# A sparse graph layer: x held for 20 tiles in five blocks, results written over x, x and out moved in blocks of four tiles

## The chip, the cores and the metric

The kernel runs on one core of a Trainium2 chip. The metric is the device time of one execution in microseconds (us). The kernel before took 1267.18 us, the median of 3 runs (1265.48 to 1268.1). All numbers are 32-bit floats.

The core has five instruction streams that run beside each other and meet at semaphores: PE (matrix products), DVE (vector work), ACT (activation functions and scaled copies), POOL (here it issues the gathers) and SP (here it issues all other transfers). Sixteen DMA engines carry the transfers of all of them.

## The reference

x is 8192 x 512, adj is 8192 x 8192. An entry of adj is nonzero with a chance of about 0.1%, and on the whole diagonal.

```python
h = jnp.maximum(_layernorm(x, axis=-1), 0.0)
head = (adj > 0).astype(adj.dtype)
head = head / jnp.maximum(jnp.sqrt(jnp.sum(head * head, axis=-1, keepdims=True)), 1e-12)
inc = adj + head
out = x + (inc @ h) / jnp.sum(inc, axis=-1, keepdims=True)
```

So every row of the result is its row of x plus a weighted mean of some nine rows of h.

## The kernel before, in words

**The tiling.** x is cut into 16 blocks of 512 rows. A block is 128 lanes of four rows in a row, so that one lane's part of a block is 8 KB that lie together in memory. A tile is one row of each lane of a block (128 rows; 2 KB in each lane, with 8 KB from lane to lane in memory), and there are 64 tiles, four to a block.

**First stage.** `ln_load` (L372) brings the blocks of x, DVE and ACT normalize them, and `ln_store` (L376) writes h to a scratch in memory. The first `HELD_CHUNKS` blocks land in `held`, which keeps them; the others land in space that the gathers use later.

**Second stage, one period for each tile t.** SP loads the tile's 128 rows of adj, 4 MB, as four transfers of 1 MB (L385) into one of two buffers. DVE folds the halves of a row together (L774), takes the eight largest of each quarter (L779) and their places (L783). From these it works out columns and weights. POOL gathers 8 rows of h for each lane by slot (L488, `slot_column`), and further rows, the spill, by 3 more transfers (L488, `spill_column`). PE multiplies them by diagonal and spill matrices and adds them up in one of three accumulators `acc`. The last three tiles and a batch of rows that the quick way missed go slightly other ways.

**The order is written out by hand.** Each engine has a `period(t)` with the steps of several tiles: DVE and ACT search and check tile t, while weights of t-1, products of t-2 and the spill of t-3 and t-4 are done in between. PE's period begins with `product_spill(t-4)` (L1341), then `residual(t-2)`, which starts the accumulator with x by a product with the unit matrix (L1318), then `bring_spill(t-2)` (L1301), on whose result DVE's `find_entry` (L941) waits one period later.

**Where x is used again.** A tile's rows of x are needed twice: by PE's `residual`, and by ACT's `row_again` (L642), which rebuilds the tile's own rows of h. For tiles 0 to 15 they come from `held`. For the 48 others `load_x(t)` (L392) brings 256 KB into one of two buffers `x_residual`, two periods ahead; it waits until PE and ACT have used the tile two before.

**The way out.** ACT's `finish_tile(t)` (L649) copies the accumulator to one of two buffers `out_tile`, once the store of two tiles before has landed. SP's `store_tile(t)` (L396) writes it, 256 KB, as a part of period t+4.

**SP's queue.** All transfers but the gathers go through SP in one order. In period t: quarters 0 and 1 of adj tile t+2, the store of tile t-4, the load of x for tile t, quarters 2 and 3. A quarter is issued when ACT has checked it in tile t and DVE has folded it. What waits at SP's head holds all that is behind it.

## Time and profile before

| | |
|---|---|
| median of 3 runs | 1267.18 us |
| the profiled execution, whole | 1265.03 us |
| its span in the trace | 1263.2 us |
| DVE busy | 1162.8 us, 92% |
| ACT and PE busy | 977.8 and 970.4 us, 77% each |
| POOL busy | 764.9 us, 61% |
| moved by the DMA engines | 471.29 MB, 373 GB/s over the span |

How to read it: the span is the time between the first and the last instruction of the trace. The 1.83 us between span and whole execution are start and end. Busy shares are means over three stages. The first 100 us are the normalization, some 100 to 1150 us are the tiles' periods, and the rest is the end, where the last tiles drain. In the second stage DVE and the DMA engines are both near their limits.

### The profile page before, as it was taken

Reading aid. Unit: us, or ns where it says so; the run is one execution under the profiler, and the core shown is the slowest. Engines: PE = TensorE matmul, PEld = TensorE weight load, DVE = VectorE, ACT = ScalarE, POOL = GpSimd, SP = SyncE. Lnnn points to the kernel's source line nnn. Section 1 sums busy time; section 2 is a strip of 40 time slices with the busy share of each in tenths; the row PEclk is TensorE's granted clock in tenths of the full one; section 3 lists DMA queues with packets and bytes.
Section 4 is the critical chain, followed back from the end, with each engine's and each line's share of the span. In section 5 each row is a group of like instructions: output and inputs, shape, how many; then the busy total and the mean of one; then the engine's idle time right before and its main releaser. Section 6 shows DMA issues by size and latency. Waiting matters only on the chain.

```text
span 1263.2 us, 14630 instructions
## 1 busy us (share of the span) xinstructions
PE 970.4 (77%) x2678; PEld 482.8 (38%) x2678; DVE 1162.8 (92%) x2794; ACT 977.8 (77%) x1903; POOL 764.9 (61%) x745
## 2 busy tenths in 40 slices
PE   0002889988888888888888888798888878878676
PEld 0001334444444434444433444344444434434343
DVE  6679999999999999999998999989999989998972
ACT  6657888898888887888887787788878778876551
POOL 1003666766666667676666666775666667667453
PEclk9999999888889999889988988988899889998698
DMA  9999999999999999999999999999999999999442
GB/s 360 428 421 406 398 402 392 392 394 399 396 391 402 401 399 398 384 401 394 384 398 368 400 398 391 388 395 373 402 400 400 385 382 387 398 399 355 142 143 79
DMA packets 148127, 471.29 MB, mean 373 GB/s; under 512 B 24386, under 2 KB 24386, under 8 KB 143876
## 3 DMA queue, kind: packets, MB, share of 16 engines
q1 hardware_dynamic: 90368, 331.38, 66.9%
q0 software_dynamic: 57664, 138.93, 29.9%
q8 instruction: 25, 0.41, 0.1%
q14 instruction: 70, 0.57, 0.1%
HBM read 490.21 MB, written 33.82 MB: 415 GB/s over the span
## 4 chain that ended last, share of the span: by engine, by line
DVE 45%; DMA 20%; issue 20%; ACT 5%; SPq 5%; another core or an unknown queue 2%; PE 1%; DVEq 0%; ACTq 0%; POOL 0%; POOLq 0%
DMA adj_tile<-in_adj_dram 17%; DVE folded L774 15%; DVE cand_word L779 12%; DVE cand_index L783 5%; DMA gathered_rows<-in_x_dram 3%; SPq L385 2%; ACT junk L569 2%; DVE cand_word L797 2%; SPq L392 2%; DVE cand_index L802 2%; ACT adj_tile L556 2%; SPq L396 1%; DVE ln_stats L757 1%; DVE weights_and_payload L914 1%
## 5 line engine op out<-in xcount | busy, mean ns | idle before, releaser
L488 POOL DMA_INDIRECT gathered_rows<-h_scratch,slot_column x520 | 536.8, 1032 | 265.9 <-issue 161.2
L569 ACT ACTIVATE junk<-adj_tile,zero_unit 128x2048 bf16<-128x2048 f32 x256 | 510.1, 1994 | 111.2 <-issue 75.5
L1330 PE MATMUL acc<-gathered_rows,diag 128*128 128x512 f32 x1040 | 504.1, 641 | 0.5 <-issue 0.5
L488 POOL DMA_INDIRECT gathered_rows<-h_scratch,spill_column x197 | 220.5, 1119 | 199.0 <-ACT spill_column L615 150.8
L774 DVE SCALAR_TENSOR_TENSOR folded<-adj_tile 128x1024 f32<-128x1024 f32 x248 | 301.4, 1215 | 12.1 <-DMA adj_tile<-in_adj_dram 10.7
L1330 PEld LDWEIGHTS acc<-gathered_rows,diag 128*128 128x128 f32 x1040 | 213.7, 212 | 247.1 <-issue 246.8
L779 DVE MAX8 cand_word<-folded 128x8 f32<-128x1024 f32 x248 | 302.9, 1221 | 2.2
L783 DVE FIND_INDEX8 cand_index<-cand_word,folded 128x8 uint32<-128x1024 f32 x248 | 302.2, 1218 | 0.0
L1341 PE MATMUL acc<-gathered_rows,spill_matrix 128*128 128x512 f32 x394 | 186.3, 607 | 14.6 <-issue 10.7
L632 ACT ACTIVATE diag<-ident,weights_and_payload 128x128 f32<-128x128 f32 x582 | 176.2, 387 | 0.5 <-DVE weights_and_payload L914 0.5
L1278 PE MATMUL poff<-spill_rank,lanes_before 128*128 128x1 f32 x130 | 26.4, 272 | 187.5 <-DVE spill_rank L859 174.4
L1278 PEld LDWEIGHTS poff<-spill_rank,lanes_before 128*128 128x128 f32 x130 | 25.4, 227 | 239.8 <-issue 139.7
L1341 PEld LDWEIGHTS acc<-gathered_rows,spill_matrix 128*128 128x128 f32 x394 | 73.9, 194 | 103.0 <-issue 102.9
L1323 PE MATMUL acc<-own_row,diag 128*128 128x512 f32 x124 | 75.2, 691 | 45.4 <-ACT own_row L642 29.2
L1307 PE MATMUL pturned<-ident,owner 128*128 128x128 f32 x394 | 79.2, 355 | 0.0
L1301 PE MATMUL pbrought<-weights_and_payload,owner 128*128 128x72 f32 (+1 forms) x386 | 71.4, 333 | 3.5 <-ACT owner L607 3.3
L1307 PEld LDWEIGHTS pturned<-ident,owner 128*128 128x128 f32 x394 | 68.8, 257 | 0.0
L615 ACT ACTIVATE spill_column<-entry 128x3 uint32<-128x3 f32 (+1 forms) x65 | 12.8, 198 | 72.3 <-issue 44.1
L1318 PE MATMUL acc<-x_residual,ident 128*128 128x512 f32 x96 | 53.2, 637 | 17.9 <-issue 14.3
L1301 PEld LDWEIGHTS pbrought<-weights_and_payload,owner 128*128 128x128 f32 x386 | 62.5, 239 | 5.9 <-ACT owner L607 4.5
L623 ACT ACTIVATE spill_matrix<-pturned,entry 128x128 f32<-128x128 f32 x197 | 56.6, 356 | 3.9 <-remote 3.9
L1323 PEld LDWEIGHTS acc<-own_row,diag 128*128 128x128 f32 x124 | 23.1, 211 | 88.1 <-ACT diag L632 46.0
(146 smaller groups left out, 829.8 us busy)
## 6 DMA issues: line engine op xcount, KB each, us to landing
adj_tile<-in_adj_dram SPq DMA_DIRECT2D x256, 1024.0 KB
h_scratch<-adj_tile SPq DMA_DIRECT2D x16, 1024.0 KB, 10.5
out_dram<-out_tile SPq DMA_DIRECT2D x64, 256.0 KB
gathered_rows<-in_x_dram SPq DMA_DIRECT2D x12, 1024.0 KB, 12.6
x_residual<-in_x_dram SPq DMA_DIRECT2D x48, 256.0 KB
gathered_rows<-h_scratch,slot_column POOLq DMA_INDIRECT x520
x_held<-in_x_dram SPq DMA_DIRECT2D x4, 1024.0 KB, 7.9
gathered_rows<-h_scratch,spill_column POOLq DMA_INDIRECT x197
```

Of the source, the lines that this page charges most:

```text
L488: nc.gpsimd.indirect_dma_start(out=into, out_offset=None, in_=h[:, :], in_offset=bass.IndirectOffsetOnAxis(ap=column, axis=0), bounds_chec ...
L569: nc.scalar.activation(junk[:, n % 2].rearrange("p (j c) -> p j c", j=2), both[:, :, half], ACT.Relu, bias=zero_unit[:], scale=-UP, accum_ ...
L623: last = nc.scalar.activation(W[:, t % 2, g], pturned[:, g * P:(g + 1) * P], ACT.Copy, scale=entry[:, t % 2, g, 0:1])
L632: last = nc.scalar.activation(diag[:, t % 2, s], ident[:], ACT.Copy, scale=wpay[:, t % 2, s:s + 1])
L774: nc.vector.scalar_tensor_tensor(out=F[:, j % 2], in0=a[:, 1], scalar=UP, in1=a[:, 0], op0=ALU.mult, op1=ALU.add).then_inc(folded, 1)
L779: nc.vector.max(out=cv[:, t % 2, 8 * j:8 * j + 8], in_=F[:, j % 2]).then_inc(vals_found, 1)
L783: nc.vector.max_index(out=ci[:, t % 2, 8 * j:8 * j + 8], in_max=cv[:, t % 2, 8 * j:8 * j + 8], in_values=F[:, j % 2]).then_inc(idx_found, 1)
L1301: last = nc.tensor.matmul(bank[:, c:c + 3 * n], owner[:, g * P:(g + 1) * P], wpay[:, t % 2, 1 + OWN:1 + OWN + 3 * n], start=True, stop=True)
L1307: last = nc.tensor.matmul(pturned[:, g * P:(g + 1) * P], owner[:, g * P:(g + 1) * P], ident[:], start=True, stop=True)
L1323: nc.tensor.matmul(acc[t % 3][:], diag[:, t % 2, 0], again[:], start=False, stop=False).then_inc(row_added, 1)
L1330: last = nc.tensor.matmul(acc[t % 3][:], diag[:, t % 2, 1 + s], slot(t % 2, s), start=False, stop=False)
L1341: last = nc.tensor.matmul(acc[t % 3][:], W[:, t % 2, g], slot(t % 2, OWN + g), start=False, stop=(g == groups(t) - 1))
```

## The change

- `held` grows from 16 to 20 tiles (five blocks), and `x_residual` and `out_tile` go. A tile's x always lies in `held[:, t % 20]`.
- `finish_tile` writes the result over the tile's x in `held`. It waits for no store any more. The batch's result goes to `again`.
- The store is of a whole block: 1 MB, 8 KB in a row in each lane, issued by SP in every fourth period, from t = 8. It waits until the block's four tiles are finished.
- x comes again in whole blocks as well, for blocks 5 to 15, eleven transfers of 1 MB. Block c+5 goes over block c and waits until the store of c has landed; SP issues it two periods after that store. So the loads lie in periods 10, 14, ... 50.
- PE tells nobody any more that x is used (`res_added` is gone).

```diff
-    HELD_CHUNKS = 4
+    HELD_CHUNKS = 5
...
-        held = sb("x_held", [P, HELD, D], fp32)
-        xres = sb("x_residual", [P, 2, D], fp32)
+        held = sb("x_then_out", [P, HELD, D], fp32)
         again = sb("own_row", [P, D], fp32)
-        osb = sb("out_tile", [P, 2, D], fp32)
...
         def x_of(t):
-            return held[:, t] if t < HELD else xres[:, t % 2]
+            return held[:, t % HELD]
+        def group(c):
+            k = c % HELD_CHUNKS
+            return held[:, ROWS * k:ROWS * (k + 1), :]
+        def out_of(t):
+            return again[:] if t == BATCH else held[:, t % HELD]
+        def x_come(t):
+            c = t // ROWS
+            return x_loaded[c % 2], 16 * ((c - HELD_CHUNKS) // 2 + 1)
...
-            def load_x(t):
-                if t >= HELD + 2:
-                    sp.wait_ge(res_added, t - 1)
-                    if not wide(t - 2):
-                        sp.wait_ge(row_ready, t - 1)
-                sp.dma_start(xres[:, t % 2], x_t[t // ROWS, t % ROWS]).then_inc(x_loaded[t % 2], 16)
-            def store_tile(t):
-                sp.wait_ge(out_ready, t + 1)
-                sp.dma_start(out_t[t // ROWS, t % ROWS], osb[:, t % 2]).then_inc(out_stored[t % 2], 16)
+            def load_x(c):
+                sp.wait_ge(out_stored[(c - HELD_CHUNKS) % 2], 16 * ((c - HELD_CHUNKS) // 2 + 1))
+                sp.dma_start(group(c), x_ln[c]).then_inc(x_loaded[c % 2], 16)
+            def store_group(c):
+                sp.wait_ge(out_ready, ROWS * c + ROWS)
+                sp.dma_start(out_ln[c], group(c)).then_inc(out_stored[c % 2], 16)
...
-                if t >= 4:
-                    store_tile(t - 4)
-                if t >= HELD:
-                    load_x(t)
+                if t >= 2 * ROWS and t % ROWS == 0:
+                    store_group(t // ROWS - 2)
+                if t % ROWS == 2 and HELD_CHUNKS <= t // ROWS - 2 + HELD_CHUNKS < LN:
+                    load_x(t // ROWS - 2 + HELD_CHUNKS)
...
-            for t in range(TILES - 4, TILES):
-                store_tile(t)
+            for c in range(LN - 2, LN):
+                store_group(c)
...
             def finish_tile(t):
                 act.wait_ge(acc_ready, t + 1)
-                if t >= 2:
-                    act.wait_ge(out_stored[t % 2], 16 * (t // 2))
-                nc.scalar.activation(osb[:, t % 2], acc[t % 3][:], ACT.Copy).then_inc(out_ready, 1)
+                nc.scalar.activation(out_of(t), acc[t % 3][:], ACT.Copy).then_inc(out_ready, 1)
```

In `row_again` and `residual` the wait for `x_loaded` takes its semaphore and count from `x_come(t)`. The compute engines keep their orders; what moves stands in SP's queue. Before, around the period in which the first x is loaded again (a quarter of adj is one L385, and `out_ready` is ACT's finished tile):

```order
L385 DMA adj_tile<-in_adj_dram 128x2x1024 [waits folded,checked] x4
L396 DMA out_dram<-out_tile 128x512 [waits out_ready]
L392 DMA x_residual<-in_x_dram 128x512
L385 DMA adj_tile<-in_adj_dram 128x2x1024 [waits folded,checked] x4
L396 DMA out_dram<-out_tile 128x512 [waits out_ready]
L392 DMA x_residual<-in_x_dram 128x512
L385 DMA adj_tile<-in_adj_dram 128x2x1024 [waits folded,checked] x4
L396 DMA out_dram<-out_tile 128x512 [waits out_ready]
L392 DMA x_residual<-in_x_dram 128x512 [waits row_ready,res_added]
L385 DMA adj_tile<-in_adj_dram 128x2x1024 [waits folded,checked] x4
```

Now, from the second tile's quarters to the second store (the first rows are periods 0 to 8; `out_stored` is the store's landing):

```order
L389 DMA adj_tile<-in_adj_dram 128x2x1024 [waits folded,checked] x34
L398 DMA out_dram<-x_then_out 128x2048 [waits out_ready]
L389 DMA adj_tile<-in_adj_dram 128x2x1024 [waits folded,checked] x8
L394 DMA x_then_out<-in_x_dram 128x2048 [waits out_stored0]
L389 DMA adj_tile<-in_adj_dram 128x2x1024 [waits folded,checked] x8
L398 DMA out_dram<-x_then_out 128x2048 [waits out_ready]
```

Two transfers of 256 KB between four quarters of adj have become one transfer of 1 MB between eight, a store and a load by turns, and eight quarters stand between a store and the load that waits for its landing.

On ACT, before, in a period of the second stage (L649 is `finish_tile`, L642 is `row_again`):

```order
L569 ACTIVATE junk,zero_units<-adj_tile,zero_unit 128x2048 [waits adj_loaded13,adj_loaded12,checked]
L649 ACTIVATE out_tile<-acc1 128x512 [waits out_stored1,acc_ready]
L593 ACTIVATE half_minus_offset<-poff 128x1 [waits places_paid,reach_ready,offset_ready]
L594 ACTIVATE spill_end<-poff,spill_rank 128x1
L600 ACTIVATE from_first_place<-place_number,half_minus_offset 128x384 [waits owner_found,minus_ready]
```

And now, at the same place:

```order
L571 ACTIVATE junk,zero_units<-adj_tile,zero_unit 128x2048 [waits adj_loaded13,adj_loaded12,checked]
L649 ACTIVATE x_then_out<-acc1 128x512 [waits acc_ready]
L595 ACTIVATE half_minus_offset<-poff 128x1 [waits places_paid,reach_ready,offset_ready]
L596 ACTIVATE spill_end<-poff,spill_rank 128x1
L602 ACTIVATE from_first_place<-place_number,half_minus_offset 128x384 [waits owner_found,minus_ready]
```

Nothing has moved there; the wait of L649 for a store is gone.

## Rows read from the trace of the kernel before

**Rows 1.** The page, part 1: busy us, share of the span, instructions of each engine.
```profile
PE 970.4 (77%) x2678; PEld 482.8 (38%) x2678; DVE 1162.8 (92%) x2794; ACT 977.8 (77%) x1903; POOL 764.9 (61%) x745
```
**Rows 2.** Stretches: busy us (instructions) of PE, PEld, DVE, ACT, POOL; clock, DMA share, GB/s.
```profile
100.00:350.00 250.00, 202.76 (x564) 102.39 (x565) 248.46 (x585) 210.97 (x410) 164.22 (x158) 0.92 1.02 397
350.00:400.00 50.00, 45.58 (x132) 22.91 (x131) 49.69 (x117) 42.57 (x85) 34.09 (x34) 0.93 1.02 395
400.00:1150.00 750.00, 640.58 (x1761) 316.88 (x1760) 718.76 (x1689) 612.91 (x1206) 506.11 (x474) 0.90 1.02 392
1000.00:1050.00 50.00, 42.67 (x114) 21.24 (x114) 44.89 (x107) 39.85 (x80) 33.68 (x33) 0.90 1.01 378
1050.00:1100.00 50.00, 43.47 (x124) 21.75 (x122) 49.69 (x118) 41.53 (x80) 33.73 (x33) 0.93 1.03 400
```
**Rows 3.** SP in time, before x is loaded again: start, us, instruction, count.
```profile
209.31 0.36 SPq L396 DMA_DIRECT2D out_dram<-out_tile  x1
...
226.00 0.36 SPq L396 DMA_DIRECT2D out_dram<-out_tile  x1
228.70 12.40 SPq L385 DMA_DIRECT2D adj_tile<-in_adj_dram  x4
```
**Rows 4.** SP in time, later, a period with a load of x.
```profile
741.64 2.07 SPq L396 DMA_DIRECT2D out_dram<-out_tile  x1
743.80 1.77 SPq L392 DMA_DIRECT2D x_residual<-in_x_dram  x1
745.67 11.66 SPq L385 DMA_DIRECT2D adj_tile<-in_adj_dram  x4
```
**Rows 5.** Waits from 150 to 1150 us: waiter, releaser, us in total, times, longest.
```profile
DVE own_entry L941 <- remote: 13.0, 3, 5.0
...
ACT half_minus_offset L593 <- remote: 11.5, 3, 4.4
...
DVE folded L774 <- DMA adj_tile<-in_adj_dram: 6.8, 9, 1.5
...
PE acc L1318 <- DMA x_residual<-in_x_dram: 3.5, 3, 1.8
```
**Rows 6.** ACT in time, 1018 to 1024 us; in brackets the idle time before.
```profile
1018.36 0.57 ACT L649 ACTIVATE out_tile<-acc 128x512 f32<-128x512 f32 x1
1023.34 0.17 ACT L593 ACTIVATE half_minus_offset<-poff 128x1 f32<-128x1 f32 x1 [4.40 <-remote]
```
**Rows 7.** The chain of waits, 930 to 975 us: start, us, what.
```profile
939.71 24.45 DMA adj_tile<-in_adj_dram
```
**Rows 8.** The page, part 6: DMA issues, count, KB each.
```profile
out_dram<-out_tile SPq DMA_DIRECT2D x64, 256.0 KB
...
x_residual<-in_x_dram SPq DMA_DIRECT2D x48, 256.0 KB
```
**Rows 9.** The page, part 3: SP's queue: packets, MB, share of 16 engines.
```profile
q1 hardware_dynamic: 90368, 331.38, 66.9%
```
**Rows 10.** The same queue from 20 to 60 us (blocks of x and h only).
```profile
q1 hardware_dynamic: 2347, 17.06, 101.1%
```
**Rows 11.** SP's queue and the gathers' from 100 to 350 us.
```profile
q1 hardware_dynamic: 18859, 69.33, 70.6%
q0 software_dynamic: 12316, 29.72, 31.7%
```
**Rows 12.** POOL in time: the last spill gather of a period.
```profile
719.28 1.36 POOL L488 DMA_INDIRECT gathered_rows<-h_scratch,spill_column  x1 [0.30 <-issue]
```
**Rows 13.** PE in time: the product that waits for it.
```profile
727.08 2.81 PE L1341 MATMUL acc<-gathered_rows,spill_matrix 128*128 128x512 f32 x6
```
**Rows 14.** Line L396: count, duration ns min/median/max, first and last start.
```profile
L396 SPq DMA_DIRECT2D out_dram<-out_tile x64: 332/734/3240, 159.3 to 1249.0; - x64
```
**Rows 15.** The chain of waits, from 1240 us.
```profile
1253.88 0.61 ACT out_tile L649
```
**Rows 16.** The chain of waits, first 10 us: a block of x, 1 MB, with no other transfer done.
```profile
0.80 4.84 DMA x_held<-in_x_dram
```

More of the change, by code:

```diff
@@ L66, in add_graph_layer @@
     x_ln = x.rearrange("(c p j) d -> c p j d", p=P, j=ROWS)
-    x_t = x.rearrange("(c p j) d -> c j p d", p=P, j=ROWS)
-    out_t = out.rearrange("(c p j) d -> c j p d", p=P, j=ROWS)
+    out_ln = out.rearrange("(c p j) d -> c p j d", p=P, j=ROWS)
     adj_h = adj.rearrange("(c p j) (h n) -> c j p h n", p=P, j=ROWS, h=2)
@@ L314, in add_graph_layer @@
         spill_gathered = [sem(f"spill_gathered{b}") for b in range(2)]
-        res_added = sem("res_added")
         row_added = sem("row_added")
@@ L422, in _ @@
                     load_chunk(t + 2, 3)
-            for t in range(TILES - 4, TILES):
-                store_tile(t)
+            for c in range(LN - 2, LN):
+                store_group(c)
             for b in range(2):
-                sp.wait_ge(out_stored[b], 16 * (TILES // 2))
+                sp.wait_ge(out_stored[b], 16 * (LN // 2))
             sp.wait_ge(list_ready, 1)
@@ L434, in _ @@
                     sp.dma_start(A[:, 0, :], adj[bass.ds(row, P, step=ROWS), :]).then_inc(d_adj, 16)
-                    sp.dma_start(xres[:, 0], x[bass.ds(row, P, step=ROWS), :]).then_inc(d_x, 16)
+                    sp.dma_start(held[:, 0], x[bass.ds(row, P, step=ROWS), :]).then_inc(d_x, 16)
                     for c in range(NCH):
@@ L440, in _ @@
                     sp.wait_ge(d_out, j + 1)
-                    sp.dma_start(out[bass.ds(row, P, step=ROWS), :], osb[:, 0]).then_inc(d_stored, 16)
+                    sp.dma_start(out[bass.ds(row, P, step=ROWS), :], held[:, 1]).then_inc(d_stored, 16)
                     sp.wait_ge(d_stored, j * 16 + 16)
@@ L536, in _ @@
             for b in range(2):
-                pool.wait_ge(out_stored[b], 16 * (TILES // 2))
+                pool.wait_ge(out_stored[b], 16 * (LN // 2))
             pool.wait_ge(out_ready, BATCH + 1)
@@ L540, in _ @@
                 out=out[:, :], out_offset=bass.IndirectOffsetOnAxis(ap=bad_row[:, 0:1], axis=0),
-                in_=osb[:, 0], in_offset=None,
+                in_=out_of(BATCH), in_offset=None,
                 bounds_check=N - 1, oob_is_err=False).then_inc(batch_stored, 16)
@@ L639, in row_again @@
                 if t >= HELD:
-                    act.wait_ge(x_loaded[t % 2], 16 * x_turn(t))
+                    act.wait_ge(*x_come(t))
                 c, j = t // ROWS, t % ROWS
@@ L1265, in _ @@
                     dve.wait_ge(d_x, j * 16 + 16)
-                    nc.vector.scalar_tensor_tensor(out=osb[:, 0], in0=pdense[:], scalar=drd[:], in1=xres[:, 0],
+                    nc.vector.scalar_tensor_tensor(out=held[:, 1], in0=pdense[:], scalar=drd[:], in1=held[:, 0],
                                                    op0=ALU.mult, op1=ALU.add).then_inc(d_out, 1)
@@ L1316, in residual @@
                 elif t >= HELD:
-                    pe.wait_ge(x_loaded[t % 2], 16 * x_turn(t))
-                nc.tensor.matmul(acc[t % 3][:], ident[:], again[:] if t == BATCH else x_of(t), start=True,
-                                 stop=False).then_inc(res_added, 1)
+                    pe.wait_ge(*x_come(t))
+                nc.tensor.matmul(acc[t % 3][:], ident[:], again[:] if t == BATCH else x_of(t), start=True, stop=False)
                 if not wide(t):
```

2 lines of the change are left out of this document (removed).

## The prediction, made before the changed kernel was run

> **What bounds the kernel now.** I read the page's busy times first. DVE is busy for 92% of the span and no other engine for more than 77% [rows 1], so DVE is the first suspect. A mean says nothing of stages, so next I cut the span into stretches [rows 2]. From 100 to 350 us DVE is busy for 248.46 of 250 us, 99.4%: it is the bound, and a gap of 0.6% is what its instructions leave between them. From 400 to 1150 us it is busy for 718.76 of 750 us. At 99.4% it would be 745.4, so 26.6 us are lost there. They come in lumps: 44.89 of 50 us from 1000 to 1050, and the full 49.69 from 1050 to 1100.
>
> What sets in after 350 us? Tile 16 is the first whose x must be loaded again. SP's queue shows what that does. Before it, a store is handed over in 0.36 us, and SP then waits until the next quarter of adj may go [rows 3]. Later the same hand-over takes 2.07 us, that of x 1.77, and the next quarters follow at once [rows 4]: SP's queue is full and SP is held by it. The DMA engines are busy at a share of 1.02 in both stretches [rows 2], so the share doesn't tell them apart; SP's hand-over time does. The waits then name the forms in which the loss reaches DVE and ACT [rows 5]: quarters of adj that come late (6.8 us), PE's brought entries that come late (13.0 us in three waits), and behind these ACT steps that start late (11.5 us in three, one of 4.40 us right behind a finished tile [rows 6], whose cause the trace doesn't name). PE waits for x by name only 3.5 us. The chain of waits passes through quarters of adj that need 24.45 us from issue to landing [rows 7].
>
> So: up to about 360 us DVE is the bound and the DMA engines just keep up. From then on the DMA engines are the bound, by a little. A period in which DVE rules is 16.69 us by the spacing of SP's stores, 226.00 minus 209.31 [rows 3]. The 750 us hold about 43.4 periods (750 minus 26.6, by 16.69), so each is 26.6 / 43.4 = 0.61 us too long: the DMA engines need 17.30 us for a tile with its x and its store.
>
> **What the change takes from the DMA engines.**
> - Bytes: x comes again for 44 tiles instead of 48, 1.05 MB less of 471 MB.
> - Packets: 48 + 64 = 112 transfers of 256 KB [rows 8] with 2 KB in a row are 14336 packets. They become 11 + 16 = 27 transfers of 1 MB with 8 KB in a row, 3456 packets: 10880 fewer. SP issues 400 transfers in all; their data packets by the access patterns are 83968 (65536 of 4 KB for adj, 4096 of 8 KB, 14336 of 2 KB), and the queue counts 90368 [rows 9], so every transfer adds 16 small ones. 85 transfers fewer are 1360 of these. Together 12240 fewer.
>
> What is a packet worth? The trace has stretches of different mix. SP's queue from 20 to 60 us, almost all 8 KB: 101.1% of 16 x 40 us is 647 us of engine time for 17.06 MB, 37.9 us per MB at 138 packets per MB [rows 10]. From 100 to 350 us, 4 KB for the most part: 2824 us for 69.33 MB, 40.7 us per MB at 272 [rows 11]. That gives 2.8 us for 134 packets, 21 ns each. The gathers of the same 250 us: 1268 us for 29.72 MB, 42.7 us per MB at 414 [rows 11], which against SP's queue gives 1.9 us for 142 packets, 14 ns each. The second pair is taken in one and the same stretch, under one load, so I take 14 ns. The upper end is 21 ns. The lower end is 0: the first pair also differs in what runs beside it, and neither pair holds a 2 KB packet by itself.
>
> The Trainium skill, "DMA: Bandwidth & Descriptors", section "Why small descriptors are slow", speaks against so large a price: it gives about 3 cycles for a packet inside a DMA engine, and the same page an 850 MHz fabric, so 3.5 ns as an estimate. The rows show 14 and 21 ns between mixes, so the trace doesn't agree so far, but it doesn't isolate the packet either. With 3.5 ns the gain below would be about 4 us.
>
> **The sum.** In the second stage each tile has, per tile, 2 x (128 - 32) = 192 data packets and 2 x 16 - 16 / 2 = 24 small ones fewer, 216 x 14 ns / 16 engines = 0.19 us. The excess over DVE's period falls from 0.61 to 0.42 us. It now falls on 44 tiles (periods 10 to 53) instead of 48: the fifth block moves the start of the loading, and the ten last periods have none. 44 x 0.42 = 18.5 us. Before, loading began at 360 us and from 350 to 400 DVE still has its 49.69 us [rows 2], so about four periods, 2.4 us, were absorbed by what had been loaded ahead. The same lead is there again: 16.1 us remain of 26.6. Gain 10.5 us.
>
> With 0 ns a packet: 44 x 0.61 - 2.4 = 24.4, gain 2.2 us. With 21 ns: 44 x 0.33 - 2.4 = 12.1, gain 14.5 us.
>
> What lies beside other work and costs nothing:
> - ACT's copy over x and PE's product keep their size, and ACT and PE are busy for 77%. Nothing reads a tile's x after its accumulator is done.
> - ACT's wait for a store goes. No row names it as the one that ended last, so it is worth 0.
> - SP's added wait, a load of block c+5 for the landing of store c: two periods, 33 us, lie between the two issues, and a transfer in the full queue needs about 24.5 us [rows 7]. So 9 us are to spare. If they were not, every quarter of adj behind would be held, and DVE after it.
> - x now lies in `held` some 12 periods before it is used, where the load had been issued two periods before. The 3.5 us of named waits go [rows 5], but they are one form of the same lack and not added.
> - First stage: the fifth block lands in `held` instead of the gathers' space. The stores of h pace those loads. 0.
>
> **The end.** The last store is issued at 1249.0 us [rows 14]; the batch's result is finished at 1254.5 [rows 15], and POOL sends it after both. The last store grows from 256 KB to 1 MB. Alone, 1 MB needs 4.84 us [rows 16], so it lands at 1253.9, in time; beside the last gathers it may need up to 3 us more, a cost of 0 to 2.4. I take 0.5, since the nearest row is the lone transfer.
>
> Total: 10.5 - 0.5 = 10.0 us. Against the profiled execution that is 1265.03 - 10.0 = 1255.0. The median of the runs shown lies 2.15 above it, so I forecast 1267.18 - 10.0 = 1257.2 us.
>
> **The rivals.**
> - *A packet costs next to nothing.* Then only the bytes and the four tiles count: 2.2 - 0.5, or 1265.5 us. For it: no row isolates a 2 KB packet. Against it: both pairs of rows give 14 ns or more. Chance 0.13.
> - *The loss is not the engines' throughput but late x and the small buffers around it.* Then it goes wholly: 26.6 us, at most 1240.6 us. For it: the loss begins with the loads of x, and two tiles of lead are little against 24.5 us of latency. Against it: SP is held in handing over adj as well, which a late x alone wouldn't do. Chance of ending below 1249: 0.12.
> - *The bursts stall DVE.* A period with a block's transfer asks for 0.75 MB more than a mean one. A tile without x and store needs 17.30 less 2 x 0.7 = 15.9 us of DMA time (262 KB at 43 us per MB by 16 engines is 0.7), one with a block 15.9 + 2.5 = 18.4, so 1.7 us over DVE's period. If nothing is given back in the light periods, 22 such periods cost 38 us instead of 26.6: 1267.2 + 11.4 = 1278.6 us. It decides when the lead of the adj loads is under 1.7 us. Against it: quarters are in flight for 24 us, and in a light period the full queue gains 0.8 us again. Chance 0.07.
> - *Gathers wait behind large packets.* If an engine takes packets of both queues by turns, a gather waits 8 KB x 37.9 us per MB = 0.31 us for each of its own instead of 0.17, for the 8 packets that an engine has of a block: 1.1 us, in 27 transfers. The last spill gather is handed over at 720.6 and its product starts at 727.1 [rows 12, 13], so several us are to spare in a calm period, but none in the three lumps. If half of the bursts meet no slack, 15 us are added, 1272 us. Chance 0.05. The skill's same page, "Queues, rings and completion order", says that an engine goes round its queues packet by packet; no row shows the turn itself.
>
> **How the numbers follow.** Forecast (a gain between 3 and 18 us) 0.63; the others 0.13, 0.12, 0.07, 0.05. The measurement tells 0.2%, 2.5 us, from no change. Faster: 0.63 + 0.12 + 0.02 of the first rival = 0.77. Within 0.2%: 0.11. Slower: 0.12 from the two last. The forecast's own range is 1249 to 1264. The range of eight in ten takes in the first rival and part of the second: 1247 to 1267.
>
> **What would show it.** Right: DVE's busy time from 400 to 1150 us rises to some 730 to 738 of 750; SP's queue holds about 78100 packets and some 330 MB; the cost per MB of that queue falls in the second stage; SP is still held in its hand-overs of adj from about 270 us on; the x loads' waits are gone. Wrong: DVE's busy time stays near 719 with fewer packets (a packet was cheap, or the lumps have a cause of their own); SP's load of a block waits for the store's landing; adj is waited for in every fourth period; or POOL's last send moves behind the last store.

## The result: 0.5% slower, and the profile after

The changed kernel took 1273.06 us, the median of 5 runs (1269.94 to 1274.22), against 1267.18 us before (5 runs by now, 1263.14 to 1268.1, the same median): a ratio of 1.0047, 95% interval 1.0027 to 1.0066. Forecast were 1257.2 us and a range of 1247 to 1267. Put on other chips beside the kernel before, the changed kernel had 1.0018 (1.0007 to 1.0030) and 1.0030 (1.0008 to 1.0051). The three intervals overlap, the first two barely; the times differ by up to 16 us, since the chips differ (below). So it is slower by 2 to 6 us, where 10 us less were forecast.

The page of the changed kernel, parts 1 and 3. It answers to [rows 1, 9].

```profile
span 1271.3 us, 14427 instructions
...
PE 974.2 (77%) x2677; PEld 486.8 (38%) x2678; DVE 1163.8 (92%) x2794; ACT 976.3 (77%) x1903; POOL 772.2 (61%) x745
...
DMA packets 135886, 470.23 MB, mean 370 GB/s; under 512 B 23026, under 2 KB 23026, under 8 KB 128180
...
q1 hardware_dynamic: 78128, 330.32, 66.0%
```

The packets are as counted, 78128 on SP's queue, and the engines' time for that queue fell: 66.0% of 1271.3 us is 839.1 us, against 66.9% of 1263.2, 845.1 us [rows 9]. That is 6.0 us of DMA time less, and the span is 8.1 us longer. So the DMA engines have less to do, and DVE still waits longer. Stretches of the changed kernel, columns as in [rows 2]:

```profile
100.00:350.00 250.00, 204.77 (x571) 102.07 (x572) 248.46 (x583) 208.34 (x399) 164.10 (x158) 0.92 1.02 394
350.00:400.00 50.00, 42.31 (x119) 21.43 (x117) 48.88 (x115) 40.69 (x84) 34.84 (x31) 0.90 1.03 401
400.00:1150.00 750.00, 637.23 (x1751) 320.31 (x1752) 711.39 (x1665) 609.71 (x1203) 507.68 (x472) 0.88 1.01 388
...
1100.00:1150.00 50.00, 44.43 (x125) 21.51 (x124) 49.69 (x118) 42.53 (x85) 34.18 (x33) 0.90 1.01 379
```

From 350 to 400 us DVE now loses time (48.88 instead of 49.69), from 400 to 1150 it has 711.39 us instead of 718.76 [rows 2], and from 1100 to 1150 it has its full 49.69 us at 379 GB/s. At 99.4% DVE would have 745.4 us from 400 to 1150, so it loses 34.0 us there, where the prediction's sum had 16.1 for the whole stage. The kernel before, from 1100 to 1150 us, lost 0.6 us, with more bytes moved:

```profile
1100.00:1150.00 50.00, 43.00 (x118) 21.80 (x119) 49.10 (x120) 42.80 (x85) 33.78 (x32) 0.86 1.02 396
```

The shortage starts earlier. In both traces it ends before the stage does: the last big wait of DVE is over at 1029 us before the change (the ACT step ahead of it is in [rows 6]) and at 1072 us now, and the tiles that follow run at DVE's own pace. The waits of the changed kernel from 150 to 1150 us, answering to [rows 5]:

```profile
DVE own_entry L941 <- remote: 14.9, 4, 5.1
ACT junk L571 <- DMA adj_tile<-in_adj_dram: 14.9, 10, 3.5
ACT half_minus_offset L595 <- remote: 11.1, 4, 4.9
...
DVE folded L774 <- issue: 6.4, 7, 1.7
```

The forms are the same as before; PE's named wait for x is gone. In this trace the lumps sit at the block transfers: ACT stands from 745, 851 and 1061 us, and SP began a block at 742, 850 and 1059. (In `after_third` it stands from 1071 and 1110 us with the last block begun at 1058, so it isn't a rule.) SP in time, 736 to 756 us (start, us, instruction), answering to [rows 4]:

```profile
741.08 0.88 SPq L389 DMA_DIRECT2D adj_tile<-in_adj_dram  x2
742.01 6.72 SPq L394 DMA_DIRECT2D x_then_out<-in_x_dram  x1
752.94 1.60 SPq L389 DMA_DIRECT2D adj_tile<-in_adj_dram  x2
```

ACT in the same stretch, answering to [rows 6]:

```profile
744.64 0.57 ACT L649 ACTIVATE x_then_out<-acc 128x512 f32<-128x512 f32 x1
750.11 0.17 ACT L595 ACTIVATE half_minus_offset<-poff 128x1 f32<-128x1 f32 x1 [4.89 <-remote]
```

SP needs 6.72 us to hand over one block of x; ACT then stands for 4.89 us at the same step as before.

**The end.** The chain of waits of the changed kernel, from 1250 us (start, us, what), answering to [rows 15]:

```profile
1250.39 6.42 DMA gathered_rows<-h_scratch,spill_column
1256.81 0.14 issue
1256.94 5.47 PE acc L1340 x6
...
1262.44 0.61 ACT own_row L649
```

The last block is stored from 1250.91 us, half a microsecond after this gather. In this execution the gather took 6.42 us and the last product waited for it. In a later execution of the same kernel (`after_third`) the chain's end passes from product to product without such a wait, and its stretch from 1250 us is like that of [rows 15]:

```profile
1253.25 2.59 PE acc L1340 x6
1255.84 0.02 issue
1255.86 0.61 ACT own_row L649
```

So the end may cost between nothing and a few us; these are two executions on two chips.

### The profile page after: what moved, and what is told of

Same layout as the page of the kernel before. It is cut to its first block, busy times and chain, and to the rows that moved or that the text cites. A ratio compares the mean times of both kernels' runs of the same rounds, so it can differ in the third digit from the quotient of the medians.

```text
span 1271.3 us, 14427 instructions
## 1 busy us (share of the span) xinstructions
PE 974.2 (77%) x2677; PEld 486.8 (38%) x2678; DVE 1163.8 (92%) x2794; ACT 976.3 (77%) x1903; POOL 772.2 (61%) x745
## 3 DMA queue, kind: packets, MB, share of 16 engines
q1 hardware_dynamic: 78128, 330.32, 66.0%
## 4 chain that ended last, share of the span: by engine, by line
DVE 49%; issue 25%; DMA 12%; ACT 9%; another core or an unknown queue 3%; SPq 1%; PE 0%; DVEq 0%; ACTq 0%; POOL 0%; POOLq 0%
DVE folded L774 17%; DVE cand_word L779 13%; DMA adj_tile<-in_adj_dram 8%; DVE cand_index L783 6%; ACT junk L571 3%; DMA gathered_rows<-in_x_dram 3%; ACT adj_tile L558 2%; ACT diag L634 1%; DVE cand_index L802 1%; DVE cand_word L797 1%; DVE diagonal_entry L827 1%; DVE weights_and_payload L914 1%; DVE ln_stats L757 1%; DVE entry_value L818 1%
## 5 line engine op out<-in xcount | busy, mean ns | idle before, releaser
L490 POOL DMA_INDIRECT gathered_rows<-h_scratch,slot_column x520 | 542.4, 1043 | 265.3 <-issue 158.3
L1340 PE MATMUL acc<-gathered_rows,spill_matrix 128*128 128x512 f32 x394 | 190.9, 622 | 14.4 <-DMA gathered_rows<-h_scratch,spill_column 11.5
L1318 PE MATMUL acc<-x_then_out,ident 128*128 128x512 f32 x128 | 68.9, 617 | 3.4 <-issue 3.4
```

Source lines behind the costliest of these rows:

```text
L490: nc.gpsimd.indirect_dma_start(out=into, out_offset=None, in_=h[:, :], in_offset=bass.IndirectOffsetOnAxis(ap=column, axis=0), bounds_chec ...
L1318: nc.tensor.matmul(acc[t % 3][:], ident[:], again[:] if t == BATCH else x_of(t), start=True, stop=False)
L1340: last = nc.tensor.matmul(acc[t % 3][:], W[:, t % 2, g], slot(t % 2, OWN + g), start=False, stop=(g == groups(t) - 1))
```

## The experiments

The kernel before took 1255.1, 1255.5, 1262.1 and 1262.4 us on the four chips used here, so times are compared on one chip and otherwise as ratios to the kernel before on the same chip. All differences below are against the changed kernel's code. Where a diff shows only the loop of SP, the semaphores' counts go with it. The expectations in us of the first group were worked out on the first chip (1267.18 us for the kernel before) and are compared here as ratios.

The theories, in short. A: the 1 MB transfers in one period (bursts) cost the time. B: packets of 8 KB hold up the gathers and the quarters of adj. C: it is the new place of the loads, ten periods earlier. D, made after the first group: time is lost in the periods in which adj, a store and a load of x share the DMA engines, and a load behind the last load of adj costs nothing. D2 adds that loads which end early leave room that nobody uses.

### First: how x and out are moved (one chip, 1262.39 us for the kernel before)

`tiles_spread`: single tiles again, one store and one load in a period, x in 20 tiles and out over x.

```diff
-                if t >= 2 * ROWS and t % ROWS == 0:
-                    store_group(t // ROWS - 2)
-                if t % ROWS == 2 and HELD_CHUNKS <= t // ROWS - 2 + HELD_CHUNKS < LN:
-                    load_x(t // ROWS - 2 + HELD_CHUNKS)
+                if t >= 4:
+                    store_tile(t - 4)
+                if HELD <= t - 10 + HELD < TILES:
+                    load_x(t - 10 + HELD)
```

> Keeps x in 20 tiles and the result written over x, but moves single tiles again (256 KB, 2 KB in a row): a store in every period (tile t-4) and a load of x in every period from 10 to 53. Theory A (the 1 MB transfers in one period stall the engines) expects the loss against the kernel before to go and the four tiles' and the long lead's gain to appear: 1260 to 1266 us. Theory B (8 KB packets hold up the gathers and the quarters of adj) expects the same here, 1260 to 1266, since both are undone. Theory C (it is the new place of the loads, ten periods earlier and nearer to full queues, whatever their shape) expects 1270 to 1275 as in the changed kernel.

`tiles_burst`: the same transfers, but four in one period.

```diff
+                if t >= 2 * ROWS and t % ROWS == 0:
+                    for j in range(ROWS):
+                        store_tile(t - 2 * ROWS + j)
+                if t % ROWS == 2 and HELD <= t - 10 + HELD < TILES:
+                    for j in range(ROWS):
+                        load_x(t - 10 + HELD + j)
```

> As the changed kernel in its periods, but each block is moved as four transfers of 256 KB with 2 KB in a row, all four in one period. Theory A (burst) expects the loss to stay, and with 10880 packets more to grow: 1273 to 1282 us. Theory B (8 KB packets) expects it to go: 1260 to 1266.

`lanes_spread`: blocks in four parts of 32 neighbouring lanes, one part in each period.

```diff
+                lanes = slice(P // 4 * k, P // 4 * (k + 1))
-                sp.dma_start(out_ln[c], group(c)).then_inc(out_stored[c % 2], 16)
+                sp.dma_start(out_ln[c][lanes], group(c)[lanes]).then_inc(out_stored[k], 16)
```

> As the changed kernel, 8 KB in a row, but every block is moved in four parts of 32 lanes (256 KB each), one part in each period, stores and loads of x alike. Theory A (burst) expects the loss to go and the packets' gain to come: 1253 to 1262 us. Theory B (8 KB packets) expects no change against the changed kernel: 1270 to 1275. Theory C expects 1270 to 1275 too.

`blocks_late`: block transfers behind the four quarters of adj.

```diff
+                    load_chunk(t + 2, 2)
+                    load_chunk(t + 2, 3)
                 if t >= 2 * ROWS and t % ROWS == 0:
                     store_group(t // ROWS - 2)
...
-                    load_chunk(t + 2, 2)
-                    load_chunk(t + 2, 3)
```

> As the changed kernel, but the store or the load of a block is issued after the four quarters of adj of its period and not between the second and the third. Theory A in its narrow form (quarters 2 and 3 of the same period are late because 1 MB stands ahead of them) expects 1 to 6 us less than the changed kernel, 1267 to 1272 us. Theory A in its wide form (1 MB more in the queue, wherever) and theory B expect the same as the changed kernel, 1270 to 1275.

| kernel | median us | ratio, 95% interval |
|---|---|---|
| tiles_spread | 1264.92 | 1.0019 (1.0002 to 1.0035) |
| tiles_burst | 1271.98 | 1.0077 (1.0052 to 1.0101) |
| blocks_late | 1265.28 | 1.0021 (1.0008 to 1.0033) |
| lanes_spread | 1332.05 | 1.0549 (1.0530 to 1.0567) |

Same transfers, same packets, four in one period instead of one: 7.1 us more, and the intervals don't overlap. That is in theory A's range (1.005 to 1.012 as a ratio), and far above theory B's, which expected 2 KB packets to end the loss. So large packets that hold up gathers, the prediction's last rival, are not the cause. But taking the burst away leaves 1.0019, not a gain, where A had expected 0.994 to 0.999: x in 20 tiles, 4 tiles fewer to load, and still not faster than before. Something else had to be found. `lanes_spread` fits no theory; it is taken up below. `blocks_late` (1.0021, where the narrow theory A had 1.000 to 1.004 and the wide one 1.002 to 1.006) is no slower than spread tiles, though it too moves 1 MB at a time. It doesn't stand beside the changed kernel on this chip, so how much the place in the period is worth is not measured.

A stretch of `tiles_burst`:

```profile
400.00:1050.00 650.00, 539.52 (x1505) 272.87 (x1506) 617.30 (x1446) 526.28 (x1040) 444.14 (x406) 0.90 1.02 389
1050.00:1150.00 100.00, 82.84 (x229) 40.39 (x227) 89.36 (x213) 77.71 (x158) 64.69 (x62) 0.93 0.96 358
```

In the second row DVE has lost 10 of 100 us and the DMA engines are at a share of 0.96 and 358 GB/s. Most of that is one wait, DVE's for a step of ACT, which itself stands for 4.38 us (start, us, instruction, in brackets the idle time before):

```profile
1090.13 0.17 ACT L600 ACTIVATE half_minus_offset<-poff 128x1 f32<-128x1 f32 x1 [4.38 <-remote]
1090.34 0.24 DVE L924 SCALAR_TENSOR_TENSOR weights_and_payload<-spill_rank,half_minus_offset,entry_sign 128x24 f32<-128x24 f32 x1 [7.05 <-ACT half_minus_offset L600]
```

While DVE stands, no buffer comes free for the next quarters of adj (SP waits for `folded` and `checked`). So the low rate there doesn't show that a burst leaves the DMA engines dry, and the 7.1 us may hold some of these ACT lumps.

### Second: when x is loaded (one chip, 1255.11 us for the kernel before)

Counting periods in the traces led to theory D. In the changed kernel DVE's steps follow at 16.68 us until 383 us (tile 17) and again from some 1072 us on. In the kernel before the loss begins at 500 us (tile 24), some four periods after the first load of x, and its last lump is over at 1029 us, so this pair shows that the loss goes with the start of the loads and says nothing on their end.

`after_again`: the changed kernel, not edited.

> The changed kernel itself once more, so that it stands on one chip beside the three others. All theories expect 1.003 to 1.007 times the kernel before.

`tiles_jit`: as `tiles_spread`, but tile t's x is loaded in period t, from 20 to 63.

```diff
                 if t >= 4:
                     store_tile(t - 4)
-                if HELD <= t - 10 + HELD < TILES:
-                    load_x(t - 10 + HELD)
+                if t >= HELD:
+                    load_x(t)
```

> x in 20 tiles and the result over x, single tiles of 256 KB, a store of tile t-4 in every period, but the load of x as late as in the kernel before: tile t's in period t, from 20 to 63. Theory D: the second stage loses some 0.8 us in every period in which adj, a store and a load of x share the DMA engines, whatever the packets; loads that fall behind the last load of adj (period 61) cost nothing. The kernel before has 46 such periods (16 to 61), the changed one 44 and single tiles loaded early 44 (10 to 53) and then wastes six or more periods in which nothing is short. Then this kernel has 42 and gains 4 x 0.8 = 3 us against the kernel before: ratio 0.996 to 0.999. The rival E, that the result written over x or the larger tile itself costs time, expects what single tiles loaded early had, a ratio of 1.001 to 1.003.

`tiles_jit_defer`: and the last 20 tiles are stored at the end.

```diff
-                if t >= 4:
+                if 4 <= t < TILES - HELD + 4:
                     store_tile(t - 4)
...
-            for t in range(TILES - 4, TILES):
+            for t in range(TILES - HELD, TILES):
                 store_tile(t)
```

> As the one before it, but the stores of the last 20 tiles are issued after the last loads, when the DMA engines are half idle. Theory D: only periods 20 to 47 carry a store and a load, 28 instead of 46, so 18 x 0.75 = 13 us less than the kernel before, less a lead that is already counted: ratio 0.988 to 0.993. Rival F, that the loss comes from the loads of x alone (their latency) and not from the sum of the traffic, expects the same as the kernel before it in this list: 0.996 to 1.003.

`blocks_no_x`: the changed kernel without its loads of x in the second stage and the two waits for them (its result is wrong).

```diff
                 if t % ROWS == 2 and HELD_CHUNKS <= t // ROWS - 2 + HELD_CHUNKS < LN:
-                    load_x(t // ROWS - 2 + HELD_CHUNKS)
+                    pass
```

> The changed kernel without the eleven loads of x in the second stage; tiles 20 to 63 then use what lies in the buffer, so the result is not the reference's. The 1 MB stores stay. Theory D expects nearly the whole loss to go, about 30 us against the changed kernel: ratio to the kernel before 0.975 to 0.983. If 1 MB in one period stalled the engines by itself (theory A as a sum over bursts, 1.7 us each), the 14 stores in the stage would leave 10 us or more: 0.984 to 0.990.

| kernel | median us | ratio, 95% interval |
|---|---|---|
| after_again | 1257.27 | 1.0018 (1.0007 to 1.0030) |
| tiles_jit | 1251.34 | 0.9974 (0.9961 to 0.9986) |
| tiles_jit_defer | 1248.66 | 0.9954 (0.9940 to 0.9967) |
| blocks_no_x | 1231.19 | 0.9811 (0.9798 to 0.9825) |

`blocks_no_x` answers the largest question: without the eleven loads 26 us go against `after_again`, most of the loss. The traffic of x on top of adj, gathers and stores is what DVE waits for, as the prediction had it. That it is the traffic and not a late x, the changed kernel shows: x is issued ten periods before its use there, PE's wait for it is gone, and the kernel is no faster. So the prediction's second rival, late x and small buffers (at most 1240.6 us), falls too. `after_again` itself had 1.0018 and so missed its range of 1.003 to 1.007 below. `tiles_jit` is the same kernel as `tiles_spread` with the loads ten periods later, and it is faster than the kernel before, as theory D says. Rival E (the result written over x costs something by itself) falls.

`tiles_jit_defer` is faster again, by 2.7 us and not by the 10 that theory D gave; its 0.9954 lies between the ranges of D (0.988 to 0.993) and of rival F (0.996 to 1.003). Its stretches, against those of `tiles_jit`, say why. `tiles_jit`:

```profile
400.00:1050.00 650.00, 563.61 (x1538) 282.28 (x1537) 623.14 (x1462) 528.70 (x1045) 447.07 (x411) 0.89 1.02 391
1050.00:1150.00 100.00, 85.22 (x235) 42.45 (x234) 96.70 (x228) 80.84 (x159) 69.60 (x65) 0.91 1.02 394
```

`tiles_jit_defer`:

```profile
400.00:1050.00 650.00, 567.32 (x1550) 284.72 (x1549) 627.97 (x1473) 533.13 (x1053) 448.97 (x413) 0.89 1.02 391
1050.00:1150.00 100.00, 86.53 (x242) 43.88 (x241) 99.13 (x239) 83.78 (x166) 71.14 (x68) 0.90 1.02 388
```

DVE gains 4.8 and 2.4 us, 7.2 us together, by the stores that are gone, and the whole kernel keeps some 3 of them. Periods with a load and no store still lose something, though periods with a store and no load lose nothing. The rest goes in the last 100 us, where the twenty stores now lie beside the last gathers: from 1150 us on PE's product waits 4.1 us for a spill gather instead of 1.9. That is a part of it; the rest isn't traced to a wait.

### Third: place of the loads once more, and 8 KB in a row without bursts (one chip, 1255.46 us for the kernel before)

`tiles_spread_again`: as `tiles_spread`.

> The kernel with single tiles loaded early (periods 10 to 53) once more, to stand on one chip beside the others. Theory D2: 44 loads cost what they cost, wherever they lie before period 61, but loads that end early let the lead of the adj transfers grow again where nobody needs it, some 3 us, and the last-moment loads of 2 tiles fall behind the last adj load. It expects 1.000 to 1.003 again. If the ratios differed only because the chips did, 0.996 to 0.999, as the late loads had.

`blocks_jit`: the changed kernel with its loads eight periods later.

```diff
-                if t % ROWS == 2 and HELD_CHUNKS <= t // ROWS - 2 + HELD_CHUNKS < LN:
-                    load_x(t // ROWS - 2 + HELD_CHUNKS)
+                if t % ROWS == 2 and HELD_CHUNKS <= t // ROWS + 1 < LN:
+                    load_x(t // ROWS + 1)
```

> The changed kernel with one edit: the load of block c is issued in period 4c-2 and not in 4c-10, so from 18 to 58. Transfers, packets and their place within a period stay. Theory D2 (the early end of the loads wastes lead) expects 2 to 5 us less than the changed kernel: ratio to the kernel before 0.998 to 1.001. If only bursts made the changed kernel slow, its ratio stays at 1.002 to 1.005.

`blocks_out_tiles_in`: loads as in `tiles_jit`; stores of blocks, behind the quarters, and the last five at the end.

```diff
+                if t >= HELD:
+                    load_x(t)
...
+                if t >= 2 * ROWS and t % ROWS == 0 and t // ROWS - 2 < LN - HELD_CHUNKS:
+                    store_group(t // ROWS - 2)
```

> x in 20 tiles; tile t's x loaded as a single tile in period t; stores of whole blocks (8 KB in a row) after the four quarters of a period, and the last five blocks stored at the end. Theory D2 with a small price of a packet (6 ns) expects 1 to 3 us less than single tiles with the last 20 stores at the end, which had 0.9954: 0.993 to 0.995. If a 1 MB store costs by being in one period, even behind the quarters, 0.996 to 0.999.

`lanes_comb`: as `lanes_spread`, with other lanes in a part.

```diff
-                lanes = slice(P // 4 * k, P // 4 * (k + 1))
+                lanes = slice(k, P, 4)
```

> Blocks in four parts of 32 lanes, 8 KB in a row, one part in each period, loads from period 10 on, as the kernel that lost 70 us; but a part is every fourth lane and not 32 lanes in a row. If the loss came from 32 neighbouring lanes sharing few ways into the memory of the lanes, it goes: ratio 0.997 to 1.002. If it came from what 32 lanes in one transfer do to the engines' shares or from 8 KB packets by themselves, it stays at 1.05.

| kernel | median us | ratio, 95% interval |
|---|---|---|
| tiles_spread_again | 1255.30 | 1.0005 (0.9994 to 1.0016) |
| blocks_jit | 1254.65 | 0.9995 (0.9980 to 1.0011) |
| blocks_out_tiles_in | 1253.82 | 0.9988 (0.9979 to 0.9997) |
| lanes_comb | 1253.84 | 0.9997 (0.9984 to 1.0010) |

Loads late instead of early: in single tiles 1.0005 to 0.9974, in blocks 1.0018 to 0.9995. Both pairs are on two chips on which the kernel before agrees within 0.4 us (1255.11 and 1255.46), and each is some 3 to 4 us. The intervals of the first pair are apart, those of the second (1.0007 to 1.0030 and 0.9980 to 1.0011) overlap a little. Stretches of `blocks_jit`, columns as before:

```profile
250.00:400.00 150.00, 131.38 (x370) 65.92 (x369) 149.07 (x351) 124.85 (x244) 102.26 (x100) 0.91 1.02 393
400.00:1050.00 650.00, 554.32 (x1527) 283.23 (x1526) 623.99 (x1464) 528.50 (x1055) 459.42 (x409) 0.88 1.02 393
```

The same stretches of `after_again`:

```profile
250.00:400.00 150.00, 130.76 (x369) 65.59 (x367) 148.40 (x349) 123.37 (x242) 102.59 (x97) 0.91 1.03 399
400.00:1050.00 650.00, 548.08 (x1515) 281.12 (x1516) 622.17 (x1455) 525.50 (x1042) 460.46 (x410) 0.88 1.02 391
```

With late loads DVE loses nothing up to 400 us and 1.8 us less up to 1050.

`blocks_out_tiles_in` missed theory D2's range and lies in the other, 0.996 to 0.999: a 1 MB store costs by being in one period, even behind the quarters. Its trace agrees. DVE's waits for adj from 150 to 1150 us, and two of them in time:

```profile
DVE folded L775 <- DMA adj_tile<-in_adj_dram: 21.3, 18, 4.5
...
777.85 8.15 SPq L399 DMA_DIRECT2D out_dram<-x_then_out  x1
...
812.91 1.23 DVE L775 SCALAR_TENSOR_TENSOR folded<-adj_tile 128x1024 f32<-128x1024 f32 x1 [4.53 <-DMA adj_tile<-in_adj_dram]
```

Four of the waits are over 2.8 us, at 602, 741, 813 and 952 us, each 29 to 35 us after SP began a block's store (572, 711, 778 and 923 us); in `tiles_jit_defer` the longest is 2.1 us. There is a second reason, by count alone: a block can be stored only when its fourth tile is done, so 12 tiles instead of 16 go out before the first load of x, and by theory D four tiles at 0.75 us are 3 us. The measured distance to `tiles_jit_defer` is 0.0034, 4.3 us. How it divides between the two isn't tested.

`lanes_comb` is the changed kernel with its bursts taken apart and nearly the same packets (79424 and 78128). It has 0.9997 where `after_again`, on a chip of the same speed, has 1.0018: the burst of 8 KB rows costs some 2.6 us, with intervals that overlap a little.

### Fourth: what was still open (one chip, 1262.07 us for the kernel before)

`comb_out_tiles_in`: as `blocks_out_tiles_in`, the stores in four parts of every fourth lane, one in a period.

```diff
-                if t >= 2 * ROWS and t % ROWS == 0 and t // ROWS - 2 < LN - HELD_CHUNKS:
-                    store_group(t // ROWS - 2)
+                if t >= 2 * ROWS and t // ROWS - 2 < LN - HELD_CHUNKS:
+                    store_group(t // ROWS - 2, t % ROWS)
```

> x in 20 tiles, tile t's x loaded alone in period t, stores with 8 KB in a row in four parts of every fourth lane, one part a period, the last five blocks at the end. If packets are worth 6 ns or more and spread parts cost nothing, this is the fastest: 0.992 to 0.995. If the packets' gain doesn't reach the end, 0.995 to 0.997 as single tiles with the last 20 stores at the end.

`tiles_jit_defer_again` and `after_third`: no edit.

> The fastest so far once more, beside the others on one chip: 0.994 to 0.997.

> The changed kernel once more, now beside these three on one chip: 1.001 to 1.005.

`tiles_no_x`: `tiles_spread` without its loads of x.

```diff
-                if HELD <= t - 10 + HELD < TILES:
-                    load_x(t - 10 + HELD)
```

> Single tiles stored in every period and no load of x in the second stage (tiles 20 to 63 use what lies in the buffer, so the result is not the reference's). Against the same with 1 MB stores, which had 0.9811, it tells what the 1 MB stores cost where the DMA engines are not short: 4 us or more (0.976 to 0.978) if a burst costs by itself, 0.980 to 0.983 if it costs only on top of full queues.

| kernel | median us | ratio, 95% interval |
|---|---|---|
| comb_out_tiles_in | 1258.79 | 0.9978 (0.9959 to 0.9996) |
| tiles_jit_defer_again | 1255.52 | 0.9948 (0.9924 to 0.9971) |
| after_third | 1265.46 | 1.0030 (1.0008 to 1.0051) |
| tiles_no_x | 1231.23 | 0.9760 (0.9735 to 0.9786) |

By its ratio `tiles_no_x` (which also leaves out the waits for x; its result is wrong) is in the range for "a burst costs by itself". By its time it isn't: 1231.23 us here and 1231.19 us with 1 MB stores there, while the kernel before is 7 us slower here. Two kernels on two chips can't tell which of the two comparisons holds. The traces tell a part. Stretches of `tiles_no_x`:

```profile
400.00:1150.00 750.00, 652.47 (x1819) 325.66 (x1817) 743.20 (x1755) 627.87 (x1239) 507.39 (x488) 0.90 1.00 385
```

And `blocks_no_x`:

```profile
400.00:1150.00 750.00, 645.66 (x1816) 322.63 (x1815) 738.74 (x1741) 628.23 (x1245) 528.96 (x486) 0.91 1.00 385
```

The 1 MB stores take 4.5 us of DVE's busy time from this stretch. `tiles_no_x` loses most of that lead at its end (the spans are 1229.0 and 1230.4 us), where ACT stands for 4.0 us before `bad_owner` (at 1140 us) and 4.7 us before `spill_matrix`; the kernel with 1 MB stores has no such wait, and its chip shows none in any trace (below). So a burst costs up to 4.5 us in the loop without loads of x, 2.6 us with them in 8 KB rows, and 7 us in 2 KB rows on a chip with ACT's lumps; each figure is from one pair.

`comb_out_tiles_in` missed both its ranges (0.992 to 0.995, 0.995 to 0.997) and is 3.3 us slower than `tiles_jit_defer_again` beside it, so spread parts of 8 KB rows bring nothing there. That a block is stored later would explain it; it isn't tested. The fastest kernel of all is single tiles, loaded as late as possible, with the last 20 stored at the end: 0.9954 and 0.9948 on two chips, some 6.5 us faster than the kernel before and 8.6 and 9.9 us faster than the changed one.

## Why the prediction was wrong, by its own steps

**The bound** was read rightly in the main. 26 us go when the loads of x go, so their traffic is what DVE waits for. What was read too smoothly are the lumps: 13.0 of the 26.6 us before are three waits of DVE behind a standing ACT step [rows 5], and the sum spread them over all periods as DMA time, 0.61 us each.

**The step that failed by most** is the packets' price, 14 ns, and with it "the excess over DVE's period falls from 0.61 to 0.42 us". Their number was right (78128). SP's queue on one chip with the same bytes: `lanes_comb` and `tiles_spread_again`.

```profile
span 1250.9 us, 14511 instructions
...
q1 hardware_dynamic: 79424, 330.33, 66.6%
```

```profile
span 1252.2 us, 14509 instructions
...
q1 hardware_dynamic: 89792, 330.33, 67.1%
```

66.6% of 1250.9 is 833.1 us, 67.1% of 1252.2 is 840.2: 7.1 us by 16 engines for 10368 packets, 11 ns each. The pair `after_again` (66.6% of 1255.8, 78128 packets) and `tiles_jit` (67.3% of 1249.6, 89792) gives 4.6 us for 11664, 6 ns. The changed kernel alone has 839.1 us in one execution and 836.4 in another, so each figure is good to some 4 ns. I had taken 14, and the rule of the Trainium skill, "DMA: Bandwidth & Descriptors", section "Why small descriptors are slow", gives an estimate of 3.5. The two measurements lie between, the lower one not clear of that estimate. My error was to take two mixes of reads, writes and gathers for two packet sizes. And what is saved hardly reaches the end: with the transfers spread, 8 KB rows had 0.9997 and 2 KB rows 1.0005 on one chip, 1.0 us, a difference inside the intervals. The sum had 8.3 of its 10.5 us of gain from it. It gave some 1 us.

**The step that turned the gain into a loss** is "It now falls on 44 tiles (periods 10 to 53) instead of 48", with "the ten last periods have none". Two things are wrong in it. The last loads of the kernel before, those issued behind the last load of adj in period 61, should have cost nothing, so that 4 tiles fewer were 2 fewer; this is argued, not measured. And the ten last periods without loads are no gift: there the DMA engines have room (379 GB/s where the kernel before had 396), and the lead that they rebuild is of no use to anybody. Loading ten periods early costs 3.9 us in single tiles (0.9974 to 1.0005) and eight periods early 2.9 us in blocks (0.9995 to 1.0018).

**The third** is the rival with the bursts, dismissed at 0.07 since "quarters are in flight for 24 us, and in a light period the full queue gains 0.8 us again". Four tiles of 2 KB rows in one period cost 0.0058, 7 us (`tiles_burst` against `tiles_spread`, one chip), and the changed kernel's own bursts some 2.6 us (`after_again` against `lanes_comb`, two chips). The sum had nothing for them. Nor was the rival right: without anything given back it priced them at 11 us.

**The ledger**, on the two chips on which the kernel before takes 1255 us:

| term | forecast, us | measured, us |
|---|---|---|
| x in 20 tiles, loaded as late as before (`tiles_jit`) | -2.2, with the next | -3.3 |
| loaded ten periods early (`tiles_spread_again`) | | +3.9 |
| 8 KB rows (`lanes_comb`) | -8.3 | -1.0 |
| a block in one period (`after_again`) | 0 | +2.6 |
| the end | +0.5 | in the others |
| sum | -10.0 | +2.3 |

The terms are differences of ratios over two chips, rounded, each good to about 2 us. On the first chip the changed kernel lost 5.9 us. The 3.6 us more have no term here.

**What differs from chip to chip** are the lumps behind ACT's `half_minus_offset`. The changed kernel was traced on three chips. DVE's waits in the form of [rows 5], in `after` (1273.06 us), then in `after_third` (1265.46 us):

```profile
DVE own_entry L941 <- remote: 14.9, 4, 5.1
```

```profile
DVE own_entry L941 <- remote: 7.0, 2, 4.7
```

In `after_again` (1257.27 us) there is no such row. It is so for all traces: the eight from the two chips with 1255 us have no wait of this step of ACT over 1 us from 150 to 1150 us and none of DVE's `own_entry` over 2 us; nine of the ten from the other three chips have one or more, of up to 7 us. The tenth, `tiles_no_x`, has its own at the end. So the lumps go with the slower chips. How much of the difference they make isn't shown, since the DMA engines catch up while DVE stands. But a loss read from the kernel before on such a chip mixes them with the DMA engines' shortage.

**What was rightly priced at nothing:** the copy over x, the store's wait that is gone, the load's wait for the store (no row of SP names it), and the first stage.

**What stays open.** The lumps in which ACT stands for 3.4 us and more, up to 7.2, at the step behind a finished tile, with all that it waits for done by the trace (PE's product for it ends at 740.2 us and the step starts at 750.1), are in both kernels on the slower chips and in no trace of the two others, and the runs don't tell their cause. Nor do they tell why a period with a load and no store loses time when one with a store and no load doesn't.

## What to carry to other kernels

When a loop is short of DMA time by a few per cent, ask of each transfer in which iteration it lies: one before the shortage cost nothing here, and of what one put off to the drain gives back in the loop some 3 of 7 us were kept. So take refills as late as their latency allows and put off stores that nobody waits for. Larger transfers in fewer places saved some 1 us where rows were 2 KB already, and cost more than that when the queue was full; spread them. Put the two kernels that you compare on one chip; a ratio to a third kernel doesn't make up for it when differences are 3 thousandths.

## What the runs showed of the hardware

A transfer of 32 neighbouring lanes is bad company. `lanes_spread` moves the same bytes as `lanes_comb`, with the same number of packets, and took 1332.05 us against 1253.84 (ratios 1.0549 and 0.9997). Stretches of `lanes_spread` and then of `lanes_comb`:

```profile
400.00:1150.00 750.00, 613.07 (x1624) 315.61 (x1625) 660.44 (x1540) 565.40 (x1113) 482.58 (x437) 0.86 1.01 361
```

```profile
400.00:1150.00 750.00, 641.62 (x1775) 324.50 (x1773) 721.78 (x1695) 613.29 (x1219) 521.60 (x475) 0.90 1.02 392
```

All transfers together slow down from 392 to 361 GB/s at the same share, though only some 7% of the bytes are moved that way, and the loss goes when the 32 lanes are every fourth one. The Trainium skill, "SBUF — State Buffer", section "Door 1: The DMA port swizzle", has a table by which lanes 0 to 31 reach 8 of the 16 ports. The two runs agree with that, but no row shows a port, and a second thing changes with the lanes: a part's rows lie together in memory, 256 KB in a row, in `lanes_spread`, and 8 KB in every 32 KB in `lanes_comb`. The runs don't separate the two.

The chips differ by up to 12 us for the kernel before (1255.1 to 1267.2). DVE's own pace doesn't differ: from 100 to 350 us it is busy for 248.46 us on each of the five. Two kernels without loads of x took 1231.2 us on two chips, but they are not the same kernel.
